# Attention on one core: the value products of a step in one piece of 512 query columns

## The chip, the cores and the metric
The kernel runs on one core of one Trainium2 chip. The metric is the device time of one execution in microseconds (us); of several runs the median is given. One execution was recorded by the hardware profiler, and its times are the ones read below.

## What is computed
Two layers, each an attention over a fixed context and a mixture of experts, all with a residual connection:

```python
x = x + L0_xattn(layernorm(x), ctx, ctx, 16)          # rotary positions, ALiBi bias
x = x + L0_ffn(layernorm(x), ...)                     # top-1 of 8 experts
x = x + L1_xattn(layernorm(x), ctx, ctx, Wq, bq, ...) # with projections
x = x + L1_ffn(layernorm(x), ...)                     # experts choose their tokens
# in both attentions, for 4 batches of 512 tokens and 16 heads of 16 columns:
attn = softmax(q @ k.T / 4 (+ bias)); out = attn @ v
```

Only the two attentions are touched. For each batch and head the scores are 512 x 512, and `attn @ v` sums over the 512 keys.

## The kernel before
Attention works in 16 slots (4 batches x 4 groups of 4 heads, `SLOTS`) of 4 steps each (`TB`, a block of 128 keys), 64 steps `t` in all. A step has two halves, one for each pair of heads. TensorE's program is one list in order of the steps (L656 to L662). In each half it issues, one behind the other:
- `scores` (L614, "S" later): for a block of 128 keys and all 512 queries the scores of two heads, keys on the partitions, with the rows' maxima taken off by extra rows of the product. Two matmuls on two halves of the array's rows.
- `maxima_scores` (L599, "M"): scores the other way round, queries on the partitions, for the slot that comes 8 steps (`AHEAD`) later. VectorE only takes their row maxima (`maxima`, L806).
- `weigh` (L633, "W"): for step `t - 1` the products of `vaug` (values and a column of ones) with `probs`, for the four heads side by side on four groups of 32 columns of the array, accumulated in `ps_out` over the slot's four steps. In half 0 it does query columns 0 to 255, in half 1 columns 256 to 511. The data are float32, and each such matmul is two pairs of weight load and product in the trace.
- pieces of other jobs that the schedule (`attention_schedule`) puts at this step and this half ("position" 0 or 1): the transposes of the maxima (`m`, L495, position 1 of each step divisible by 4), of the outputs (`o`, L503, position 1 of each step 4s + 7), of the normalized queries (L512, position 1), in layer 1 also the projection of the queries (`job_q1`, L520, both positions) and the output projection (L549, L557). All of them share one PSUM bank, `ps_misc`, and each waits until the one before has been copied out.

ScalarE takes exp of each S unit (L739, 128 x 1024), in order, and behind the second half of steps divisible by 4 it copies `ps_out` to `out_sb` (L745) and then the maxima to `max_t` (L674). VectorE, besides the maxima, negates them at the end of a slot (L812, L813) and divides the outputs (L784, L791).

S and M write to a ring of three units of two PSUM banks in the fixed order S, M, S, M, ... (`ring_schedule`). So each takes the unit of the one three places before (`take_unit`, L572 to L578): an M waits for the exp of the S of the half step before (`exp_done`), an S for the row maximum of the M two half steps before (`mx_read`). `weigh` waits for the second exp of step `t - 1`, and in the first step of a slot for the copy of the slot before (`out_copied`). `probs` has three buffers; an exp waits for the products of three steps before (`pv_done`).

In the first 8 steps (`t` below 0) there are only maxima, in the last 8 (56 to 63) no more maxima. Each stage of the kernel begins when the one before has ended. SyncE issues the loads of queries, keys and maxima, GpSimd the stores of the queries and keys, each waiting for counts of `st_full`, `mx_full`, `misc_free` or `pv_done`.

Of the kernel before, what the change touches and what calls it, by code (L numbers as in the profile page):

```python
# [15 lines left out]
B, T, D = 4, 512, 256  # L16
# [3 lines left out]
TB = T // P  # L20
DC = D // P
FC = F // P
HG = 4
# [3 lines left out]
VW = 32  # L27
# [116 lines left out]
def attention(nc, m, layer, dram):  # L144
# [7 lines left out]
    NV = 2 if layer == 0 else B  # L152
    with ExitStack() as ctx:
        def sb(name, shape, dt):
            return ctx.enter_context(nc.sbuf_tensor(f"a{layer}_{name}", shape, dt))

        def sem(name):
            return m.ctx.enter_context(nc.semaphore(f"a{layer}_{name}"))
# [3 lines left out]
        probs = sb("probs", [P, 3, HG, T], F32)  # L162
        vaug = sb("vaug", [P, NV, TB, H, VW], F32)
# [44 lines left out]
        vaug_set = sem("vaug_set")  # L208
# [14 lines left out]
        exp_done = sem("exp_done")  # L223
        v_ready = sem("v_ready")
        pv_done = sem("pv_done")
        out_copied = sem("out_copied")
# [80 lines left out]
        with nc.Block() as block:  # L307
# [182 lines left out]
            def _(pe):  # L490
# [73 lines left out]
                def piece(job, n):  # L564

                    if n == 0 and index[job] and not (layer == 1 and job in first):
                        pe.wait_ge(misc_free, index[job])
                    ins = run[job[0]](job, n)
                    if n == last_piece.get(job[0], 0):
                        ins.then_inc(misc_full, 1)  # L570
# [9 lines left out]
                def maxima_scores(n):  # L580

                    if not 0 <= n < 2 * STEPS:
                        return
                    s, w = n // 8, n % 8
                    p, qt = w // TB, w % TB
                    b, g = s // NG, s % NG
                    for part in range(2 if b else 3):
                        if w == 0 and g == groups(b, part)[0]:
                            if s == 0:
                                pe.wait_ge(first_loaded, 64)  # L590
                            else:
                                pe.wait_ge(loaded[part if b else part - 1], 64 * (b + 1))
                            if s in row_pieces:
                                piece = row_pieces.index(s)
                                pe.wait_ge(rows_in[piece % 2], 32 * n_kinds * (piece // 2 + 1))
                    to = take_unit("m", n)
                    for par in range(2):
                        rows = slice(par * HALF_P, par * HALF_P + M_ROWS)
                        ins = pe.matmul(to[:, par], qa[rows, b % 2, g, p, qt * P:(qt + 1) * P], ka[rows, b % 2, g, p], start=True, stop=True)  # L599
                    ins.then_inc(mx_full, 1)  # L600

                def scores(n):

                    if not 0 <= n < 2 * STEPS:
                        return
                    t, p = n // 2, n % 2
                    s, kc = t // TB, t % TB
                    b, g = s // NG, s % NG
                    if kc == 0 and p == 0:
                        pe.wait_ge(max_in[s % 2], 32 * (s // 2 + 1))  # L610
                    to = take_unit("s", n)
                    for par in range(2):
                        rows = slice(par * HALF_P, par * HALF_P + S_ROWS)
                        ins = pe.matmul(to[:, par], ka[rows, b % 2, g, p, kc * P:(kc + 1) * P], qa[rows, b % 2, g, p], start=True, stop=True)  # L614
                    ins.then_inc(st_full, 1)

                def weigh(t, half):

                    if not 0 <= t < STEPS:
                        return  # L620
                    s, kc = t // TB, t % TB
                    b, g = s // NG, s % NG
                    cols = slice(half * T // 2, (half + 1) * T // 2)
                    if half == 0:
                        pe.wait_ge(exp_done, 2 * t + 2)
                        if kc == 0:
                            pe.wait_ge(v_ready, b + 1 if layer == 0 else 2 * (b + 1))
                            if layer == 1:
                                pe.wait_ge(vaug_set, 1)
                            if s:  # L630
                                pe.wait_ge(out_copied, s)
                    for h in range(HG):
                        ins = pe.matmul(m.ps_out[VW * h:VW * (h + 1), cols], vaug[:, b % NV, kc, HG * g + h], probs[:, t % 3, h, cols],  # L633
                                        start=(kc == 0 and half == 0), stop=(kc == TB - 1 and half == 1), skip_group_check=True)
                    if half == 1:
                        ins.then_inc(pv_done, 1)

                pe.wait_ge(m.ident_in, 16)
                if layer == 1:
# [16 lines left out]
                for t in steps:  # L656
                    for half in range(2):
                        scores(2 * t + half)
                        maxima_scores(2 * (t + AHEAD) + half)
                        weigh(t - 1, half)  # L660
                        for job, n in pieces.get((t, half), []):
                            piece(job, n)  # L662

            @block.scalar
            def _(act):
                def act_job(job):
                    if job[0] in ("o", "a"):
                        return
                    act.wait_ge(misc_full, index[job] + 1)
                    if job[0] == "m":  # L670
                        s = job[1]
                        if s >= 2:
                            act.wait_ge(max_in[s % 2], 32 * (s // 2))
                        nc.scalar.copy(max_t[:, s % 2], misc[0:2 * MAX_ROWS]).then_inc(misc_free, 1)  # L674
                    elif job[0] == "qt":
                        nc.scalar.copy(xnt[:, job[1] % 2], bank(job)[:].rearrange("p (c t) -> p c t", c=DC)).then_inc(misc_free, 1)
                    elif job[0] == "q":
                        i = job[1]
                        if i >= 2:
                            act.wait_ge(q_ready, max(i - 1, 2))  # L680
                        src = bank(job)[:].rearrange("p (c t) -> p c t", c=DC)
                        if layer == 0:
                            nc.scalar.copy(qx[:, i % 2], src).then_inc(misc_free, 1)
                        else:
                            to = qst[:, i, 0] if i < 2 else qx[:, i % 2]
                            for o in range(DC):
                                ins = nc.scalar.activation(to[:, o], src[:, o], ACT.Identity, bias=bqk[:, 0, o:o + 1])
                            ins.then_inc(misc_free, 1)
                    elif job[0] == "at":
                        _, b, c = job  # L690
                        if b:
                            act.wait_ge(misc_full, index["a", b - 1, 1] + 1)
                        nc.scalar.copy(att_t[:, c], misc[:]).then_inc(misc_free, 1)
# [1064 lines left out]
```

## Time and profile before

| | us |
|---|---|
| runs, median of 3 | 1064.61 (1059.42 to 1065.59) |
| the profiled execution | 1059.8 |
| its span, from the first to the last instruction | 1058.0 |
| TensorE products busy | 951.0 |
| VectorE busy | 596.9 |
| ScalarE busy | 514.3 |
| GpSimd busy | 309.5 |

Busy times are sums over the whole span, and the stages differ in their limits. Products on TensorE overlap in the profile's records, since their ends are modelled, so that the distance between the starts of two groups says more than their lengths. A group of S, M or W in the trace in order of time is one line with its count (x2, x2, x8).

### The profile page before, as it was taken

Reading aid. Unit: us, or ns where it says so; the run is one execution under the profiler, and the core shown is the slowest. Engines: PE = TensorE matmul, PEld = TensorE weight load, DVE = VectorE, ACT = ScalarE, POOL = GpSimd, SP = SyncE. Lnnn points to the kernel's source line nnn. Section 1 sums busy time; section 2 is a strip of 40 time slices with the busy share of each in tenths; the row PEclk is TensorE's granted clock in tenths of the full one; section 3 lists DMA queues with packets and bytes.
Section 4 is the critical chain, followed back from the end, with each engine's and each line's share of the span. In section 5 each row is a group of like instructions: output and inputs, shape, how many; then the busy total and the mean of one; then the engine's idle time right before and its main releaser. Section 6 shows DMA issues by size and latency. Waiting matters only on the chain. (4 is left out here: it accounts for less than half of the span.)

```text
span 1058.0 us, 17516 instructions
## 1 busy us (share of the span) xinstructions
PE 951.0 (90%) x6902; PEld 653.6 (62%) x6902; DVE 596.9 (56%) x1011; ACT 514.3 (49%) x777; POOL 309.5 (29%) x296
## 2 busy tenths in 40 slices
PE   4289999997988999998879999999979999999994
PEld 3134344443858999998634434344349989999994
DVE  7588989981440111110796856869415846655663
ACT  1148777785342323322336765757643044445550
POOL 7597661000001222223042122000001255554222
PEclk9569999999689999999888989989998999999998
DMA  7878555200569999994737161330007225555316
GB/s 249 170 219 226 132 124 108 40 3 20 195 255 352 346 335 350 339 335 153 175 99 147 38 143 41 64 63 3 4 1 242 81 70 133 153 167 136 100 20 179
DMA packets 53045, 158.98 MB, mean 150 GB/s; under 512 B 8272, under 2 KB 28368, under 8 KB 42288
## 3 DMA queue, kind: packets, MB, share of 16 engines
q1 hardware_dynamic: 36464, 121.96, 38.8%
q0 software_dynamic: 13296, 29.63, 10.5%
q10 hardware_dynamic: 3216, 6.43, 1.6%
q8 instruction: 48, 0.79, 0.3%
q14 instruction: 21, 0.17, 0.1%
HBM read 116.18 MB, written 40.76 MB: 148 GB/s over the span
## 5 line engine op out<-in xcount | busy, mean ns | idle before, releaser
L806 DVE TENSOR_REDUCE a_row_max<-ps_ring 128x2 f32<-128x1024 f32 x256 | 308.4, 1221 | 76.9 <-PE ps_ring L599 76.2
L739 ACT ACTIVATE a_probs<-ps_ring 128x1024 f32<-128x1024 f32 x256 | 261.3, 1024 | 99.3 <-PE ps_ring L614 97.9
L633 PE MATMUL ps_out<-a_probs,a_vaug 128*32 128x256 f32 x2048 | 168.3, 402 | 2.5 <-ACT a_out_sb L745 1.5
L599 PE MATMUL ps_ring<-a_ka,a_qa 52*128 52x512 f32 (+1 forms) x512 | 120.8, 475 | 29.4 <-DMA a_ka<-scratch_k_scr 21.4
L614 PE MATMUL ps_ring<-a_qa,a_ka 56*128 56x512 f32 (+1 forms) x512 | 132.3, 513 | 2.3 <-DMA a_qa<-a_max_t 1.2
L1076 ACT ACTIVATE e_hid<-ps_ring,e_wts 128x128 f32<-128x128 f32 x184 | 52.3, 369 | 119.5 <-PE ps_ring L1176 70.0
L614 PEld LDWEIGHTS ps_ring<-a_qa,a_ka 56*128 56x128 f32 (+1 forms) x512 | 49.2, 189 | 97.0 <-issue 68.2
L1465 ACT ACTIVATE e_hr<-ps_ring 128x512 fp32r<-128x512 f32 x64 | 38.3, 599 | 118.2 <-PE ps_ring L1536 118.2
L633 PEld LDWEIGHTS ps_out<-a_probs,a_vaug 128*32 128x32 f32 x2048 | 41.0, 109 | 80.0 <-issue 73.9
L599 PEld LDWEIGHTS ps_ring<-a_ka,a_qa 52*128 52x128 f32 (+1 forms) x512 | 51.8, 200 | 61.7 <-ACT a_probs L739 22.8
L1536 PE MATMUL ps_ring<-e_xt,e_wr 128*128 128x512 f32 x384 | 88.7, 390 | 0.4 <-DVE e_xt L1604 0.4
L1176 PEld LDWEIGHTS ps_ring<-e_xst,e_wts 128*128 128x128 f32 x736 | 87.2, 195 | 2.0 <-issue 0.8
L1176 PE MATMUL ps_ring<-e_xst,e_wts 128*128 128x128 f32 x736 | 87.5, 278 | 0.6 <-DVE e_xst L1275 0.6
L1188 PE MATMUL ps_ring<-e_wts,e_hid 128*128 128x256 f32 x368 | 83.8, 381 | 0.1
L1536 PEld LDWEIGHTS ps_ring<-e_xt,e_wr 128*128 128x128 f32 x384 | 71.6, 188 | 15.1 <-issue 0.6
L1624 DVE TENSOR_TENSOR e_hr<-e_hf,e_hr 128x512 fp32r<-128x512 f32 x64 | 44.4, 694 | 54.5 <-ACT e_hf L1468 54.5
L1188 PEld LDWEIGHTS ps_ring<-e_wts,e_hid 128*128 128x128 f32 x368 | 68.1, 190 | 9.3 <-ACT e_hid L1076 0.8
L1429 POOL DMA_INDIRECT scratch_acc<-e_ys,e_token x32 | 57.1, 1786 | 54.7 <-DVE e_ys L1618 50.8
L1017 POOL DMA_INDIRECT scratch_ys<-e_ys,e_to_row x23 | 22.8, 992 | 122.0 <-DVE e_ys L1284 122.0
L1420 POOL DMA_INDIRECT e_xg<-scratch_xl,e_token x32 | 32.2, 1008 | 75.7 <-PE ps_ring L1520 46.7
L1284 DVE TENSOR_TENSOR e_ys<-ps_ring,e_wts 128x256 f32<-128x256 f32 x23 | 9.8, 424 | 75.4 <-PE ps_ring L1188 75.4
L1281 DVE TENSOR_TENSOR e_xst<-ps_misc,e_rms_t 128x256 f32<-128x256 f32 x22 | 9.3, 424 | 75.4 <-PE ps_misc L1157 75.4
(231 smaller groups left out, 1283.4 us busy)
## 6 DMA issues: line engine op xcount, KB each, us to landing
e_wts<-in_w SPq DMA_DIRECT2D x23, 1156.0 KB, 8.4
e_wts<-in_w SPq DMA_DIRECT2D x23, 1024.0 KB, 8.0
e_wf<-in_w SPq DMA_DIRECT2D x16, 1024.0 KB, 6.1
a_qa<-scratch_q_scr SPq DMA_DIRECT2D x28, 384.0 KB, 8.6
a_ka<-scratch_k_scr SPq DMA_DIRECT2D x28, 384.0 KB, 7.2
scratch_q_scr<-a_qst POOLq DMA_DIRECT2D x36, 256.0 KB, 3.2
scratch_k_scr<-a_kst POOLq DMA_DIRECT2D x9, 512.0 KB, 13.8
scratch_xl<-e_xn SPq DMA_DIRECT2D x8, 512.0 KB, 5.3
```

The costliest lines, as they stand in the source:

```text
L599: ins = pe.matmul(to[:, par], qa[rows, b % 2, g, p, qt * P:(qt + 1) * P], ka[rows, b % 2, g, p], start=True, stop=True)
L614: ins = pe.matmul(to[:, par], ka[rows, b % 2, g, p, kc * P:(kc + 1) * P], qa[rows, b % 2, g, p], start=True, stop=True)
L633: ins = pe.matmul(m.ps_out[VW * h:VW * (h + 1), cols], vaug[:, b % NV, kc, HG * g + h], probs[:, t % 3, h, cols], start=(kc == 0 and half ...
L739: nc.scalar.activation(probs[:, t % 3, 2 * half:2 * half + 2], unit("s", n), ACT.Exp, scale=HD ** -0.5).then_inc(exp_done, 1)
L806: dve.tensor_reduce(row_max[:, s % 3, qt, :, p], unit("m", n), AX.X, ALU.max).then_inc(mx_read, 1)
L1076: nc.scalar.activation(hid[:, k, fc], m.ps_st[:, 2 * k + half, q * P:(q + 1) * P], ACT.Silu, bias=wts[:, k, w1_cols + FC * D + fc:w1_cols ...
L1176: ins = pe.matmul(m.ps_st[:, 2 * k + half, q * P:(q + 1) * P], wts[:, k, c * F + fc * P:c * F + (fc + 1) * P], xst[:, k, c], start=(c == 0 ...
L1188: ins = pe.matmul(m.ps_max[:, k, 0:D], hid[:, k, fc], wts[:, k, w1_cols + fc * D:w1_cols + (fc + 1) * D], start=(fc == 0), stop=(fc == FC ...
L1429: pool.indirect_dma_start(dram["acc"], bass.IndirectOffsetOnAxis(token[:, e, b:b + 1], 0), ys[:, e % 2, b], None, compute_op=ALU.add).then ...
L1465: nc.scalar.activation(hr[:, 0, fc], m.ps_st[:, fc % 4], ACT.Gelu_apprx_tanh)
L1536: ins = pe.matmul(m.ps_st[:, fc % 4], wr[:, k, wp, c * F + fc * P:c * F + (fc + 1) * P], xt[:, xp, c], start=(c == 0 and (wp, xp) == (0, 0 ...
L1624: dve.tensor_tensor(hr[:, 1, fc], hf[:, fc % 4], hr[:, 0, fc].bitcast(F32), ALU.subtract).then_inc(h_split, 1)
```

## The change
The four heads' products of a step are issued once, in the first half of the following step, with all 512 query columns each. In the second half nothing takes their place. The waits are the same and stand where they stood, at the first half. The increment of `pv_done`, which used to come with the last product of the second half, now comes with the last of the first half. The order on TensorE was S M W S M W in a step and is S M W S M.

```diff
-                def weigh(t, half):
+                def weigh(t):
...
-                    cols = slice(half * T // 2, (half + 1) * T // 2)
-                    if half == 0:
-                        pe.wait_ge(exp_done, 2 * t + 2)
-                        if kc == 0:
...
+                    pe.wait_ge(exp_done, 2 * t + 2)
+                    if kc == 0:
...
                     for h in range(HG):
-                        ins = pe.matmul(m.ps_out[VW * h:VW * (h + 1), cols], vaug[:, b % NV, kc, HG * g + h], probs[:, t % 3, h, cols],
-                                        start=(kc == 0 and half == 0), stop=(kc == TB - 1 and half == 1), skip_group_check=True)
-                    if half == 1:
-                        ins.then_inc(pv_done, 1)
+                        ins = pe.matmul(m.ps_out[VW * h:VW * (h + 1)], vaug[:, b % NV, kc, HG * g + h], probs[:, t % 3, h],
+                                        start=(kc == 0), stop=(kc == TB - 1), skip_group_check=True)
+                    ins.then_inc(pv_done, 1)
...
                         scores(2 * t + half)
                         maxima_scores(2 * (t + AHEAD) + half)
-                        weigh(t - 1, half)
+                        if half == 0:
+                            weigh(t - 1)
                         for job, n in pieces.get((t, half), []):
                             piece(job, n)
```

## Rows read from the trace of the kernel before

**Rows 1.** The page, busy time (share of the span) and instructions of TensorE.
```profile
PE 951.0 (90%) x6902; PEld 653.6 (62%) x6902; DVE 596.9 (56%) x1011; ACT 514.3 (49%) x777; POOL 309.5 (29%) x296
```

**Rows 2.** The page's groups by line: busy us, mean ns of one | idle before.
```profile
L806 DVE TENSOR_REDUCE a_row_max<-ps_ring 128x2 f32<-128x1024 f32 x256 | 308.4, 1221 | 76.9 <-PE ps_ring L599 76.2
...
L633 PE MATMUL ps_out<-a_probs,a_vaug 128*32 128x256 f32 x2048 | 168.3, 402 | 2.5 <-ACT a_out_sb L745 1.5
```

**Rows 3.** Stretches: us, busy of each engine, granted clock, DMA share, GB/s.
```profile
200.30:211.96 11.66, 11.66 (x108) 4.74 (x104) 10.55 (x14) 9.14 (x11) 0.73 (x1) 1.00 0.02 4
234.00:255.00 21.00, 19.31 (x190) 7.08 (x188) 2.56 (x9) 17.58 (x20) 2.05 (x3) 1.00 0.02 4
```

**Rows 4.** In order of time (start us, us), layer 0, two half steps.
```profile
205.46 1.02 ACT L739 ACTIVATE a_probs<-ps_ring 128x1024 f32<-128x1024 f32 x1 [0.43 <-PE ps_ring L614]
...
206.15 0.50 PE L614 MATMUL ps_ring<-a_qa,a_ka 56*128 56x512 f32 x2
206.53 0.19 PEld L599 LDWEIGHTS ps_ring<-a_ka,a_qa 52*128 52x128 f32 x2 [0.20 <-ACT a_probs L739]
...
206.69 1.02 ACT L739 ACTIVATE a_probs<-ps_ring 128x1024 f32<-128x1024 f32 x1 [0.21 <-PE ps_ring L614]
...
206.97 0.64 PE L633 MATMUL ps_out<-a_probs,a_vaug 128*32 128x256 f32 x8
...
207.54 0.50 PE L614 MATMUL ps_ring<-a_qa,a_ka 56*128 56x512 f32 x2
...
207.88 0.39 PE L599 MATMUL ps_ring<-a_ka,a_qa 52*128 52x512 f32 x2
...
208.20 0.64 PE L633 MATMUL ps_out<-a_probs,a_vaug 128*32 128x256 f32 x8
```

**Rows 5.** The same view: steps with out transposes (L503) and maxima transposes (L495).
```profile
210.16 0.66 PE L503 MATMUL ps_misc<-ident,a_out_sb 128*128 128x128 f32 x4
...
210.74 0.50 PE L614 MATMUL ps_ring<-a_qa,a_ka 56*128 56x512 f32 x2
...
210.96 0.18 DVE L812 TENSOR_SCALAR a_neg_max<-a_row_max 128x16 fp32r<-128x16 f32 x1
...
211.89 2.34 DVE L806 TENSOR_REDUCE a_row_max<-ps_ring 128x2 f32<-128x1024 f32 x2
...
213.36 0.60 PE L495 MATMUL ps_misc<-ident,a_neg_max 128*8 128x128 f32 x4
213.56 0.59 ACT L745 COPY a_out_sb<-ps_out 128x512 f32<-128x512 f32 x1
...
213.90 0.50 PE L614 MATMUL ps_ring<-a_qa,a_ka 56*128 56x512 f32 x2
```

**Rows 6.** The same view: last eight steps of layer 0.
```profile
234.50 0.64 PE L633 MATMUL ps_out<-a_probs,a_vaug 128*32 128x256 f32 x8
...
241.62 0.64 PE L633 MATMUL ps_out<-a_probs,a_vaug 128*32 128x256 f32 x8
242.19 0.19 PEld L614 LDWEIGHTS ps_ring<-a_qa,a_ka 56*128 56x128 f32 x2 [0.41 <-issue]
...
242.74 1.02 ACT L739 ACTIVATE a_probs<-ps_ring 128x1024 f32<-128x1024 f32 x1 [0.17 <-PE ps_ring L614]
...
253.55 1.07 PE L633 MATMUL ps_out<-a_probs,a_vaug 128*32 128x256 f32 x16
```

**Rows 7.** The same view: a step of layer 1 with the query projection.
```profile
642.24 1.13 PE L520 MATMUL ps_misc<-a_xnt,a_wq 128*128 128x256 f32 x4
...
644.30 0.66 PE L503 MATMUL ps_misc<-ident,a_out_sb 128*128 128x128 f32 x4 [0.93 <-ACT a_qx L687]
```

**Rows 8.** The same view: the first value products of layer 0.
```profile
68.32 1.08 PE L633 MATMUL ps_out<-a_probs,a_vaug 128*32 128x256 f32 x8
69.33 0.79 PE L614 MATMUL ps_ring<-a_qa,a_ka 56*128 56x512 f32 x2
```

More of the change, by code:

```diff
@@ L622, in weigh @@
                     b, g = s // NG, s % NG
-                    cols = slice(half * T // 2, (half + 1) * T // 2)
-                    if half == 0:
-                        pe.wait_ge(exp_done, 2 * t + 2)
-                        if kc == 0:
[L627 to L631, printed above, removed]
+                    pe.wait_ge(exp_done, 2 * t + 2)
+                    if kc == 0:
+                        pe.wait_ge(v_ready, b + 1 if layer == 0 else 2 * (b + 1))
+                        if layer == 1:
+                            pe.wait_ge(vaug_set, 1)
+                        if s:
+                            pe.wait_ge(out_copied, s)
                     for h in range(HG):
-                        ins = pe.matmul(m.ps_out[VW * h:VW * (h + 1), cols], vaug[:, b % NV, kc, HG * g + h], probs[:, t % 3, h, cols],
-                                        start=(kc == 0 and half == 0), stop=(kc == TB - 1 and half == 1), skip_group_check=True)
-                    if half == 1:
-                        ins.then_inc(pv_done, 1)
+                        ins = pe.matmul(m.ps_out[VW * h:VW * (h + 1)], vaug[:, b % NV, kc, HG * g + h], probs[:, t % 3, h],
+                                        start=(kc == 0), stop=(kc == TB - 1), skip_group_check=True)
+                    ins.then_inc(pv_done, 1)
                 pe.wait_ge(m.ident_in, 16)
```

## The prediction
> **What bounds the kernel now.** I read the page's busy shares first: TensorE is busy 90% of the 1058.0 us span [rows 1]. The groups by line come next: the four heads' value products of L633 and the row maxima of L806 are among the costliest [rows 2], and both belong to the two attention layers. Only these are touched, so the rest of the reading is of their steps. A stretch of exactly four steps late in layer 0 is 11.66 us long, has TensorE busy all through and VectorE for 10.55 us, and the granted clock is 1.00 in it, the upper of the two levels, 2.4 GHz [rows 3]. That is 2.91 us a step.
>
> A busy TensorE is not yet one that sets the pace, so I went to the instructions in order of time [rows 4]. I call the score products of L614 S, the maxima products of L599 M, the value products of L633 W. A half step is S, M, W. The distances between starts are S to M 0.34 (207.54 to 207.88), M to W 0.32 (207.88 to 208.20), W to the next S 0.57 (206.97 to 207.54): 1.23 us. Every second half step has M held back: at 206.53 its weights are loaded, released by the exp of the S before, which ran from 205.46 to 206.48. Such a half step takes S to M 0.38 and M to W 0.44, 0.16 more. A step without other work is thus 2 x 1.23 + 0.16 = 2.62. Four of them, the out transposes (0.58, 210.16 to 210.74) and the maxima transposes (0.54, 213.36 to 213.90) [rows 5] make 11.60, against 11.66 seen. So TensorE sets the pace, in order, and one wait just begins to show: with three units in the ring, M of a half step writes where the S of the half step before was, and must wait for its exp.
>
> That wait is the one to watch. exp starts 0.54 after its S (206.15 to 206.69), takes 1.02, and M's load follows 0.05 behind its end: **1.61 us** from an S to the M it releases. Today S, M, W and the next S fill 1.23 + 0.34 = 1.57 of it, so that only 0.04 shows directly, and 0.12 because M's weights can't be loaded ahead.
>
> **The change, part by part.**
>
> *The products themselves.* Of W's 16 pairs of load and product a step, 8 of double width remain. No row shows four heads side by side at 512 columns. Bound from above: two separate pieces, 2 x 0.57 = 1.14. Nearest row: at 253.55 all 16 pairs run with nothing between, in 1.07 [rows 6] against 0.64 for 8 [rows 4]. So a second piece adds 0.43, and the fixed part is 0.57 - 0.43 = 0.14. Bound from below: the streaming alone, 0.86. The 16 pairs cost 0.57 + 0.43 = 1.00; I take 0.99 for the wide piece, which has half the loads, since these lay beside products already. TensorE's work falls by 2 x 0.57 - 0.99 = 0.15 us a step.
>
> *The order.* A step becomes S0, M0, W, S1, M1, then the next S0, M0. Between S1 and the next M0 there is no W: S1 to M1 0.34, M1 to S0 0.32, S0 to M0 0.34, 1.00 us in place of 1.57, while S1's exp still takes 1.61. So in each plain step M0 is held by 0.6 us, and W, behind it in the queue, too. The loop is M0 to W 0.44, W to S1 0.99, S1 to M0 1.61: **3.04 us** against 2.62, +0.42. M1 isn't held: it follows S1, 1.4 us behind M0, when the exp of S0 is long over.
>
> *What the gap hides.* Pieces at position 1 of `piece` lie between M1 and the next S0, in those 0.6 us. They cost their full length before. A step with the out transposes stands at +0.42 - 0.58 = -0.16 (only W's saving is left). VectorE then has the negated maxima and the division between two row maxima, 0.93 (210.96 to 211.89) [rows 5]. It is done with M1's maximum 3.42 after M0 (M1 at 1.77, start 0.43 later, 1.22 long [rows 2]), begins the next at 4.35 and ends it at 5.57; the S0 that needs this comes at 5.13 without it, so at 5.62, and its M0 0.38 later at 6.00, still ahead of 6.08 where its exp ends. No cost, with 0.08 to spare. A step with the maxima transposes: +0.42 - 0.54 = -0.12. But the copy of L745 stands on ScalarE behind S1's exp, 0.59 long [rows 5], and the next W needs its end, about 0.14 later than W would come otherwise: +0.14, so +0.02.
>
> *Steps 1 to 55 of each layer.* Layer 0: 25 plain x 0.42 = 10.5; 13 with maxima transposes x 0.02 = 0.3; 13 with out transposes and 4 with query transposes x -0.16 = -2.7. Less 0.8 for the 0.06 by which 11.60 falls short of 11.66 in 14 groups, and less 1 for the first two steps, in which the clock is at 1.2 GHz, a piece of W takes 1.08 [rows 8] and TensorE's own work covers the exp: +6.3. Layer 1 has the query projection too, 1.13 of work in each half of a step, and waits between pieces such as the 0.93 ahead of 644.30 [rows 7]. Where that work is, the new wait is covered. 22 plain x 0.42 = 9.2; 8 x 0.02 = 0.2; 10 with out transposes and 15 full ones x -0.16 = -4.0; less 0.8; less 2 for some five steps at the low clock: +2.6.
>
> *Steps 56 to 63, without maxima.* From the W at 234.50 to that at 253.55 are 19.05 us for 8 steps. A plain one is W to S 0.57 (241.62 to 242.19), S to exp 0.55, exp 1.02, next W 0.05: 2.19 [rows 6]. With W in one piece it is 0.99 + 0.55 + 1.02 + 0.05 = 2.61. Eight are 20.9; twice the copy of L745 stands between the exp and the W that needs both, +0.55 each; the transposes are hidden. 22.0 against 19.05: +2.95 a layer, 5.9 for both. The next stage begins behind the layer's last instruction, so all of it counts.
>
> **Sum:** 6.3 + 2.6 + 5.9 = +14.8 us. No DMA is moved past another: SyncE and GpSimd wait for counts of S, M and W that come within a microsecond of before, and the load of the maxima has three steps to land. The profiled execution took 1059.8 us, so the sum gives 1074.6. The median of the runs, 1064.6, is 4.8 above it; from there it is 1079.4. I take the middle, **1077 us**.
>
> **Rivals.**
> *A, TensorE stays the bound and the change wins.* If M0's wait were covered, 0.15 us would be saved in each of 126 steps: -19, 1041 on the profiled time, 1046 on the median: 1043. For it: TensorE busy in all of 11.66 us. Against: M's load is released by an exp in today's trace already. It decides where the loop of M0, W, S1 and exp is no longer than TensorE's own work of 2.62 - 0.15 = 2.47 a step, that is if the 1.61 were under 1.04. The Trainium skill, page Perfetto Trace Analysis, section Matmuls, says that larger matmuls are more efficient than smaller ones where possible; by that rule alone the time would come out as here. The trace agrees as to the 0.14 that each piece costs beside its columns, not as to what waits for it.
> *B, no change.* W takes its streaming alone, 0.86: the loop is 2.91, and 0.13 less in 126 steps is -16: -2 in all, 1058 to 1063. Within 1% it is as long as W is under 0.95.
> *C, more is late.* W costs 1.14: 0.15 x 126 = 19 more, 1096. Or the copy, the cast and the row maxima add 0.25 to 0.5 in each of 27 groups of four steps, as the 0.08 to spare is used up: 7 to 13 more, 1084 to 1090.
> *D, the clock falls.* TensorE would be at work for 2 x 0.34 + 0.99 = 1.67 of 2.61 us in the last steps, 64%; today it is for 1.82 of 2.19 and the clock is 1.00 [rows 3]. At 1.2 GHz a piece of W holds the engine for 1.01 (68.32 to 69.33) in place of 0.57, and S is 0.79 long, not 0.50 [rows 8]; the wide piece would be 0.99 x 1.01 / 0.57 = 1.75. With S1 0.29 longer and M0 0.2, the loop grows by 1.25 a step: 16 steps give +20, 1097.
>
> **From these to the numbers.** Forecast 0.58 (itself 1070 to 1085), A 0.07, B 0.13, C 0.15, D 0.07. The range 1060 to 1092 leaves out A, D and the upper end of C. About 1% is what a measurement of this kernel tells from no change, here 1054 to 1075. Slower by over 1%: three quarters of the forecast, C and D, 0.66. Within 1%: the rest of the forecast and B, 0.27. Faster: A, 0.07.
>
> **What would show it.** Four steps late in layer 0 take 12.2 to 12.4 us (4 x 3.04 + 0.14), not 11.66. In plain steps the load of M0 starts 0.05 behind an exp, and M0 about 0.95 behind S0 instead of 0.34; M1 is not held; W to S1 is 0.95 to 1.0; both transposes lie in the gap and the loop is no longer with them than without; the last steps are 2.6 apart. W to S1 below 0.9 would make B right; an M0 that no exp releases, A; a clock of 0.5 in the last steps, D.

## The result and the profile after
The changed kernel is slower: 1087.7 us median (1082.9 to 1091.0) against 1064.6 (1059.4 to 1065.6), ratio 1.024 with a 95% interval of 1.019 to 1.029. Measured twice more, beside the kernel before on the same chip each time, it gave 1.0165 (1.013 to 1.020) and 1.018 (1.015 to 1.021). The three together are about +1.95%, or +20.7 us. Runs more than 1.5% above the fastest of their kernel, which also had a lower mean clock, are left out of the ratios.

The page of the changed kernel, with the rows that answer to [rows 1, 2], and below it the one row of the kernel before that is needed beside them:

```profile
span 1089.1 us, 15468 instructions
...
PE 935.9 (86%) x5878; PEld 635.7 (58%) x5878; DVE 596.3 (55%) x1011; ACT 506.0 (46%) x777; POOL 309.9 (28%) x296
...
L804 DVE TENSOR_REDUCE a_row_max<-ps_ring 128x2 f32<-128x1024 f32 x256 | 307.3, 1221 | 95.0 <-PE ps_ring L599 93.0
...
L599 PE MATMUL ps_ring<-a_ka,a_qa 52*128 52x512 f32 (+1 forms) x512 | 121.0, 475 | 55.3 <-ACT a_probs L737 27.9
L631 PE MATMUL ps_out<-a_probs,a_vaug 128*32 128x512 f32 x1024 | 142.3, 628 | 12.9 <-ACT a_probs L737 8.1
```

```profile
L599 PE MATMUL ps_ring<-a_ka,a_qa 52*128 52x512 f32 (+1 forms) x512 | 120.8, 475 | 29.4 <-DMA a_ka<-scratch_k_scr 21.4
```

TensorE's work has fallen, from 951.0 to 935.9 us, and W's from 168.3 to 142.3, but the span grew by 31.1. TensorE is idle for 55.3 us ahead of M (L599), where it was 29.4, and the exp (L737) ends 27.9 of that; before, what ended most of it was a load of the keys. A smaller busy time with a longer span says that the work saved was not what the time hung on.

Four steps late in layer 0 of the changed kernel, by busy time (us, busy of PE, its weight load, DVE, ACT, POOL, granted clock, DMA share, GB/s), answering to [rows 3]; they begin and end at an S:

```profile
207.28:219.70 12.42, 11.10 (x76) 4.05 (x73) 10.56 (x14) 8.80 (x10) 0.74 (x1) 1.00 0.02 4
```

TensorE has 1.3 us of idle time in them, where it had none in 11.66. By the exps, whose starts mark a period more evenly, four such steps are 12.36. The instructions in order of time show where it sits, one plain step of the changed kernel, answering to [rows 4]:

```profile
212.52 1.06 PE L631 MATMUL ps_out<-a_probs,a_vaug 128*32 128x512 f32 x8
...
213.51 0.50 PE L614 MATMUL ps_ring<-a_qa,a_ka 56*128 56x512 f32 x2
...
213.85 0.40 PE L599 MATMUL ps_ring<-a_ka,a_qa 52*128 52x512 f32 x2
...
214.06 1.94 ACT L737 ACTIVATE a_probs<-ps_ring 128x1024 f32<-128x1024 f32 x2 [1.11 <-PE ps_ring L614]
214.09 0.39 PE L614 MATMUL ps_ring<-a_qa,a_ka 56*128 56x512 f32 x2
...
215.13 0.51 PE L599 MATMUL ps_ring<-a_ka,a_qa 52*128 52x512 f32 x2 [0.66 <-ACT a_probs L737]
...
215.57 1.06 PE L631 MATMUL ps_out<-a_probs,a_vaug 128*32 128x512 f32 x8
```

S1 starts at 213.51, its exp at 214.06, and M0 can begin at 215.13 only, 0.66 after TensorE was ready. W stands behind M0 in the queue and starts at 215.57. From W to W it is 3.05: 0.99 to S1, 1.62 to M0, 0.44 to W.

### The profile page after: what moved, and what is told of

The parts are those of the page before. It is cut to its first block and busy times, and to the rows that moved or that the text cites. A ratio compares the mean times of both kernels' runs of the same rounds, so it can differ in the third digit from the quotient of the medians.

```text
span 1089.1 us, 15468 instructions
## 1 busy us (share of the span) xinstructions
PE 935.9 (86%) x5878; PEld 635.7 (58%) x5878; DVE 596.3 (55%) x1011; ACT 506.0 (46%) x777; POOL 309.9 (28%) x296
## 5 line engine op out<-in xcount | busy, mean ns | idle before, releaser
L737 ACT ACTIVATE a_probs<-ps_ring 128x1024 f32<-128x1024 f32 x256 | 257.2, 1023 | 136.2 <-PE ps_ring L614 135.8
L599 PE MATMUL ps_ring<-a_ka,a_qa 52*128 52x512 f32 (+1 forms) x512 | 121.0, 475 | 55.3 <-ACT a_probs L737 27.9
L631 PE MATMUL ps_out<-a_probs,a_vaug 128*32 128x512 f32 x1024 | 142.3, 628 | 12.9 <-ACT a_probs L737 8.1
L614 PE MATMUL ps_ring<-a_qa,a_ka 56*128 56x512 f32 (+1 forms) x512 | 125.6, 494 | 5.1 <-DVE a_row_max L804 3.6
L599 PEld LDWEIGHTS ps_ring<-a_ka,a_qa 52*128 52x128 f32 (+1 forms) x512 | 51.8, 199 | 95.5 <-ACT a_probs L737 54.8
L631 PEld LDWEIGHTS ps_out<-a_probs,a_vaug 128*32 128x32 f32 x1024 | 20.9, 109 | 51.0 <-issue 33.1
```

The source lines that it names most:

```text
L631: ins = pe.matmul(m.ps_out[VW * h:VW * (h + 1)], vaug[:, b % NV, kc, HG * g + h], probs[:, t % 3, h], start=(kc == 0), stop=(kc == TB - 1) ...
L737: nc.scalar.activation(probs[:, t % 3, 2 * half:2 * half + 2], unit("s", n), ACT.Exp, scale=HD ** -0.5).then_inc(exp_done, 1)
```

## The experiments
Kernels named "wide" have W in one piece; those named "halves" have it in two. All ratios are against the kernel before, run on the same chip. "Four steps" is the mean distance of four steps over steps 36 to 51 of layer 0, by the starts of the exps; "the last eight" is the time from the first exp of step 56 to the end of the last exp of step 63, in layer 0 too. For the kernel before it is 18.9, for the changed one 21.9.

**The two kernels again.** No edit: first the kernel before, then the changed one.

> The kernel before, unchanged, profiled once more, to see how far the stages that the change does not touch differ from one execution to the next. Theory 1 (chance of the execution): the two mixtures of experts, 165.5 and 202.1 us long in the first profile of before, come out up to 3 us longer or shorter here, and the clock of an attention's first steps rises up to 3.4 us earlier or later. Theory 2 (a consequence of the change): they come out as before within 0.5 us, and only kernels with the wide piece show the 168.1 and 208.2 us.

> The changed kernel, unchanged, with its time and one more profile. Both theories: four steps late in layer 0 take 12.3 us, the wide piece is 0.99 from its start to the next score products, M0's load follows an exp. Theory 1: mixtures of experts 165 to 168 and 202 to 208, not tied to the kernel; time 1084 to 1090. Theory 2: 168 and 208 again.

Measured: before 1066.6 us (one run; 1064.7 is the median of 17 beside it), four steps 11.64, the last eight 18.86. Changed 1083.6, ratio 1.0165 (1.013 to 1.020); four steps 12.36, the last eight 24.2, with the clock at its lower level in steps 62 and 63.

The first pair of profiles differed by 31.1 us, of which 12.0 lay outside both attentions (each taken from its first exp to its last), in code that is the same. From the start of layer 1's last W to the end it was 278.8 us in the first profile of the kernel before and 285.8 in the second, and 287.8 and 286.9 in the changed kernel. Over thirteen profiles that stretch went from 278.8 to 290.2, and the one from layer 0's last W to layer 1's first exp from 291.3 to 298.4, with either form of W at both ends. So nothing ties the 12.0 to the change: executions of either kernel differ by as much, and only the steps themselves are compared below.

**Is it the width of the products or their place?** Both pieces of 256 columns, but one right behind the other at the first half:

```diff
-                        weigh(t - 1, half)
+                        if half == 0:
+                            weigh(t - 1, 0)
+                            weigh(t - 1, 1)
```

> The change's place without its size: the two pieces of 256 columns stay, but both are issued in the first half. Theory (the place costs, as M0 has to wait for S1's exp): the pair takes 1.00, the loop 3.05, four steps 12.3 to 12.4, the time within 0.3% of the changed kernel's. Rival (the width costs, a product of 512 columns over four column groups streams slower or holds back what is behind it): the time within 0.5% of the kernel before.

Measured: 1080.1 us, ratio 1.019 (1.013 to 1.025); four steps 12.38, the last eight 21.91. In order of time, this kernel:

```profile
192.91 1.07 PE L633 MATMUL ps_out<-a_probs,a_vaug 128*32 128x256 f32 x16
...
193.91 0.49 PE L614 MATMUL ps_ring<-a_qa,a_ka 56*128 56x512 f32 x2
...
195.52 0.50 PE L599 MATMUL ps_ring<-a_ka,a_qa 52*128 52x512 f32 x2 [0.60 <-ACT a_probs L741]
```

Sixteen narrow pairs hold TensorE for 1.00 us (192.91 to 193.91), eight wide ones for 0.99. The width is worth 0.01 us a step; in the steps the whole loss is in the place, and so is the saving of 0.15, since it comes whenever two pieces stand next to each other.

**The piece at the second half.** From the changed kernel:

```diff
-                        if half == 0:
+                        if half == 1:
                             weigh(t - 1)
```

> The wide piece of step t - 1 in the second half, behind S1 and M1, instead of the first: S0 M0 S1 M1 W. Theory (M waits 1.61 us for the exp of the S before, and the gap this opens is only worth something where pieces lie in it): the loop is M1, W, S0, exp, M1 and again 0.44 + 0.99 + 1.61 = 3.04, but the transposes of the second half now stand between W and S0, on the loop, and cost their 0.58 and 0.54: four steps 12.16 + 1.12 = 13.3, against 12.35 of the changed kernel, about 25 us more in all, 1105 to 1112. Rival (the loss is one of the wide piece itself): the time within 0.5% of the changed kernel's.

Measured: 1103.7 us, ratio 1.0385 (1.033 to 1.044); four steps 13.37, the last eight 16.60, less than in either kernel. In order of time, this kernel:

```profile
200.20 0.49 PE L599 MATMUL ps_ring<-a_ka,a_qa 52*128 52x512 f32 x2 [0.65 <-ACT a_probs L737]
...
200.63 1.07 PE L631 MATMUL ps_out<-a_probs,a_vaug 128*32 128x512 f32 x8
...
201.62 0.66 PE L503 MATMUL ps_misc<-ident,a_out_sb 128*128 128x128 f32 x4
...
202.21 0.50 PE L614 MATMUL ps_ring<-a_qa,a_ka 56*128 56x512 f32 x2
...
203.83 0.50 PE L599 MATMUL ps_ring<-a_ka,a_qa 52*128 52x512 f32 x2 [0.64 <-ACT a_probs L737]
```

Now W (200.63) and the transposes (201.62) stand in one half, and the other half still has its wait of 0.64 for the exp. What W's place decides is which half is left empty. With W at the first half the gap takes the transposes in; with W at the second it takes in nothing.

**M behind W.** If M0 holds W back, W could be put ahead of it. It must then be that of step t - 2, since the exp of t - 1 isn't over; the copy of `ps_out` goes one step later. From the changed kernel:

```diff
                         scores(2 * t + half)
+                        if half == 0:
+                            weigh(t - 2)
                         maxima_scores(2 * (t + AHEAD) + half)
-                        if half == 0:
-                            weigh(t - 1)
...
-                        if half == 1 and t >= TB and t % TB == 0 and t // TB <= SLOTS:
+                        if half == 1 and t >= TB and t % TB == 1 and t // TB <= SLOTS:
```

> The wide piece works on step t - 2 and stands between S0 and M0; the copy of the outputs moves one step later with it. Nothing then waits for an exp that is not long over: from S1 to the next M0 there are 2.0 us of work. Theory (a ring of three units is short of time, whichever of its waits is met): the next S0 waits for the row maximum of M0, 0.44 + 1.22 + 0.05 behind it, then 0.44 to W and 0.99: a loop of 3.14, with the delay of VectorE at a slot's end 12.8 for four steps; the last eight steps, where there are no maxima, fall to 2.0 to 2.1 each: 1083 to 1092 us. Rival (only M0's wait for exp cost time): four steps come down to VectorE's 10.7 and the kernel is faster than before, 1035 to 1045.

Measured: 1096.1 us, ratio 1.032 (1.025 to 1.038); four steps 13.26, a plain step 3.25 to 3.42, the last eight 19.19. In order of time, this kernel:

```profile
208.60 0.50 PE L599 MATMUL ps_ring<-a_ka,a_qa 52*128 52x512 f32 x2
...
209.15 2.35 DVE L804 TENSOR_REDUCE a_row_max<-ps_ring 128x2 f32<-128x1024 f32 x2 [1.07 <-PE ps_ring L599]
...
210.43 0.50 PE L614 MATMUL ps_ring<-a_qa,a_ka 56*128 56x512 f32 x2 [0.85 <-DVE a_row_max L804]
210.85 1.06 PE L631 MATMUL ps_out<-a_probs,a_vaug 128*32 128x512 f32 x8
...
211.85 0.50 PE L599 MATMUL ps_ring<-a_ka,a_qa 52*128 52x512 f32 x2
```

The wait for an exp is gone and another has taken its place: S at 210.43 is released by a row maximum that began at 209.15, and M0 at 211.85 comes 3.25 after the M0 at 208.60. W makes M0 late, M0's row maximum ends late, and the S that writes there waits. In this order the ring's other wait takes over, and it costs more than the 12.8 that were expected; whether some third order would do wasn't tried. The last eight were to fall to 2.0 to 2.1 a step. A plain step there is 1.81, but twice W waits for the copy of the outputs, 1.46 and 1.63 us, and the eight together gain nothing.

**A cut that isn't even.** From the kernel before, with `weigh` taking its first and last column: 384 columns at the first half and 128 at the second.

```diff
-                        weigh(t - 1, half)
+                        cut = 3 * T // 4
+                        if half == 0:
+                            weigh(t - 1, 0, cut)
+                        else:
+                            weigh(t - 1, cut, T)
```

> One size changed: query columns 0 to 383 in the first half, 384 to 511 in the second. Theory (loop = 2.05 + the first piece, which is 0.14 + 0.43 for each 256 columns): first piece 0.79, a plain step 2.83, between 2.62 and 3.04; four steps 11.9 to 12.1, last steps 2.4: 1073 to 1078 us. Rival (the wait appears only with one undivided piece): 2.62, the time of the kernel before.

Measured: 1070.2 us, ratio 1.007 (1.004 to 1.010); four steps 11.70, the last eight 20.35 and a plain one of them 2.40. In order of time, this kernel:

```profile
191.96 0.49 PE L599 MATMUL ps_ring<-a_ka,a_qa 52*128 52x512 f32 x2
...
192.38 0.85 PE L633 MATMUL ps_out<-a_probs,a_vaug 128*32 128x384 f32 x8
...
193.16 0.50 PE L614 MATMUL ps_ring<-a_qa,a_ka 56*128 56x512 f32 x2
...
194.78 0.18 PEld L599 LDWEIGHTS ps_ring<-a_ka,a_qa 52*128 52x128 f32 x2 [0.41 <-ACT a_probs L743]
194.78 0.49 PE L599 MATMUL ps_ring<-a_ka,a_qa 52*128 52x512 f32 x2
```

M0 to M0 is 2.82 us (191.96 to 194.78), between 2.62 and 3.04, and S1 to M0 is 1.62 again (193.16 to 194.78). W with 384 columns holds the engine 0.78. The loop of M0 to W, W to S1, S1 to M0 gives 0.42 + 0.78 + 1.62 = 2.82. The same sum gives 3.04 with the 0.99 of W whole and 2.62 with the 0.57 of a half, where it is M1 that is held: it fits all three cuts. The four steps came out 0.2 to 0.4 shorter than expected, since a step behind one with transposes doesn't wait, and the whole time came out 3 us below the 1073 to 1078 expected.

**One piece only where something fills the gap.** If the gap is what costs, W in one piece should gain in those steps where a transpose stands at the second half. From the kernel before, with `weigh` taking its first and last column:

```diff
-                        weigh(t - 1, half)
+                        cut = T if (t, 1) in pieces and t < STEPS - AHEAD else T // 2
+                        if half == 0:
+                            weigh(t - 1, 0, cut)
+                        elif cut < T:
+                            weigh(t - 1, cut, T)
```

> The wide piece only in those steps, up to step 55, in whose second half another job's piece is scheduled; elsewhere two halves as before. Theory (a gap of 0.6 us opens behind S1 and pays only where a transpose fills it): two plain steps 2.62 each, two steps with transposes 3.04 and 3.18, so 11.46 for four in place of 11.66, 0.2 less in 27 groups and some 0.2 more in each step with a query or output projection: 5 to 8 us faster than the kernel before, 0.5 to 0.7%. Rival (the wide piece costs wherever it stands): slower than before by half of what the change costs, about 1%.

Measured: 1065.1 us, ratio 1.0015 (0.999 to 1.004); four steps 11.83, the last eight 18.85. Four steps should have been 11.46. In order of time, this kernel, in the step behind maxima transposes:

```profile
200.99 0.58 ACT L749 COPY a_out_sb<-ps_out 128x512 f32<-128x512 f32 x1
...
201.93 1.92 ACT L743 ACTIVATE a_probs<-ps_ring 128x1024 f32<-128x1024 f32 x2
...
202.99 0.50 PE L599 MATMUL ps_ring<-a_ka,a_qa 52*128 52x512 f32 x2 [0.21 <-ACT a_probs L743]
```

In steps divisible by 4 ScalarE copies the outputs and casts the maxima behind S1's exp. The next exp starts only at 201.93, and the M at 202.99 waits for it. So in these steps the gap on TensorE is filled but ScalarE isn't free. The step behind them takes 3.18 from M0 to M0, although its own W is in halves, where the kernel before took 2.69. The same edit without them:

```diff
-                        cut = T if (t, 1) in pieces and t < STEPS - AHEAD else T // 2
+                        cut = T if (t, 1) in pieces and t % TB and t < STEPS - AHEAD else T // 2
```

> As the mixed kernel, but steps divisible by 4 keep their halves: there the copy and the cast on ScalarE hold back the exps behind them, and the mixed kernel paid 0.43 us. Theory: the wide piece stays where out or query transposes fill the gap, 0.16 less in 26 steps and about 0.2 in some 12 others: 5 to 7 us faster than the kernel before at the same clock, 0.5 to 0.7%. Rival (what a wide step gains, the next gives back): within 0.2% of the kernel before.

Measured: **1056.3 us** (1051.6 to 1060.0, 11 runs), ratio 0.9935 (0.991 to 0.996); four steps 11.41, the last eight 18.89. In order of time, this kernel, a step with the out transposes:

```profile
184.84 1.07 PE L633 MATMUL ps_out<-a_probs,a_vaug 128*32 128x512 f32 x8
...
186.38 1.03 ACT L743 ACTIVATE a_probs<-ps_ring 128x1024 f32<-128x1024 f32 x1 [0.64 <-PE ps_ring L614]
...
186.50 0.66 PE L503 MATMUL ps_misc<-ident,a_out_sb 128*128 128x128 f32 x4
...
187.09 0.49 PE L614 MATMUL ps_ring<-a_qa,a_ka 56*128 56x512 f32 x2
...
187.55 0.49 PE L599 MATMUL ps_ring<-a_ka,a_qa 52*128 52x512 f32 x2
```

The transposes at 186.50 lie where S1's exp runs (186.38 to 187.41), so that the M at 187.55 comes 0.46 behind its S and not 1.04 as in a plain step of the changed kernel (214.09 to 215.13). Four steps fell by 0.25. Of this 0.15 is W's own saving. Most of the rest is that M1 isn't held in such a step, since W stands whole between S0 and S1: from S1 to M1 and on to what follows it is 0.34 and 0.33, where the kernel before has 0.38 and 0.44. This version beats both kernels, by 0.65% the one before.

**Free M from S's ring.** How much of the loss hangs on the shared ring shows when it is taken away. Rings of their own, two units for S and two of one bank for M, fit in PSUM only if M is half as large. From the kernel before, the changed kernel, and the changed kernel with `weigh(t - 2)` and the copy a step later:

```diff
-            r = 2 * (place[kind, n] % 3)
+            if kind == "m":
+                return ring[:, 4 + n % 2:5 + n % 2]
+            r = 2 * (n % 2)
...
-                        pe.wait_ge(mx_read if was == "m" else exp_done, k + 1)
+                    if n >= 2:
+                        pe.wait_ge(mx_read if kind == "m" else exp_done, n - 1)
...
-                    for par in range(2):
+                    for par in range(1):
```

> Units apart: scores have two units of two banks, maxima two units of one bank. For that only one of the two maxima products is made (VectorE reads its bank twice, so its time is the same), and exp multiplies its input by zero, so that all values stay finite. The value products are in halves, as before. M no longer waits for an exp nor S for a row maximum. Expected by all: the wait behind every second S is gone, 2.46 a step, four steps 10.9 to 11.0 in place of 11.66.

> The same units apart and the same parts left out (one of two maxima products, exp of zero), with the wide piece in the first half. Theory (the change lost because M0 had to wait for S1's exp): what is left is W's own wait for that exp, a loop of 0.99 + 1.61 = 2.60, four steps 11.0 to 11.1: nearly the halves' 10.95, where with the shared ring there were 0.7 between them. Rival (the wide piece itself): 0.7 us more than with halves again, 11.6.

> As the kernel with units apart and the wide piece, but the piece works on step t - 2, so that it waits for no exp either. Theory: no wait is left but VectorE's eight maxima and 0.93 for a slot's end: 10.7 us for four steps, 0.25 less than with halves: the saving of 0.15 a step shows at last, as far as VectorE lets it. Rival: as much as with halves or more.

These kernels leave out one of the two maxima products of each half (VectorE reads its bank twice in place of it) and take exp of zero, so their whole times (1076, 1063 and 1059 us, one run each) say nothing beside the others, and their steps are compared among the three alone. Four steps: halves 10.99, wide 11.33, wide a step later 11.10. In order of time, first two W a step apart of the wide kernel, then one of the later kernel:

```profile
190.69 1.06 PE L631 MATMUL ps_out<-a_probs,a_vaug 128*32 128x512 f32 x8 [0.40 <-ACT a_probs L737]
...
193.31 1.07 PE L631 MATMUL ps_out<-a_probs,a_vaug 128*32 128x512 f32 x8 [0.40 <-ACT a_probs L737]
```

```profile
194.31 1.06 PE L631 MATMUL ps_out<-a_probs,a_vaug 128*32 128x512 f32 x8 [0.85 <-ACT a_out_sb L743]
```

The loss of wide against halves falls from 0.70 to 0.34 in four steps, and a plain step is 2.62, not 3.04. So about half of the loss in the steps goes with the ring. What is left is W's own wait: even with M free it waits 0.40 for S1's exp, which S1, pushed behind W, starts late. I had expected 11.0 to 11.1 for wide. The later kernel was to show 10.7, and showed 11.10, as W then waits for the copy of the outputs on ScalarE (0.85). That a wide W can win in every step, with both waits gone, wasn't shown.

**The clock.** In all four profiles with W joined at the first half (three of the wide kernel and that of the two pieces together) the clock falls in the last steps of layer 1, at step 59 or 62, in two of them in those of layer 0 too, and in step 53 of layer 1. The wide kernel with rings of its own does it too, at steps 59 and 53. It happens in none of the four profiles with W in halves at these steps (twice the kernel before, both mixed). At steps 21 and 37 of layer 1 the clock falls in some profiles with either form of W (both in the first of the kernel before, 37 in the second of the changed one), so there it belongs to the execution. Two stretches of layer 1, the changed kernel, columns as above:

```profile
761.00:765.00 4.00, 3.32 (x18) 1.27 (x16) 0.97 (x1) 2.20 (x3) 0.00 (x0) 0.63 0.06 12
...
785.90:789.30 3.40, 3.40 (x14) 1.14 (x14) 0.00 (x0) 1.58 (x2) 0.00 (x0) 0.51 0.02 5
```

The third number from the end is the clock, 0.63 and 0.51 of full speed, the second being the lower level, 1.2 GHz. The step at the first took 7.68 us against 5.83 in the kernel before, by the exps of S1; that at the second took 3.75 against 2.61 in the changed kernel's second profile, where the clock hadn't fallen yet. The idle time alone doesn't settle it: the last steps of layer 0 have the same gaps, and in two of the four profiles the clock stays at its upper level in them. To see whether the idle time brings this on, products were repeated in the gap (S0 again, in each step that has no transposes ahead of it), from the changed kernel:

```diff
-                    for par in range(2):
...
+                    again = 0 if p or not t or (t - 1, 1) in pieces else 2 if t > STEPS - AHEAD else 1
+                    for _ in range(1 + again):
+                        for par in range(2):
...
```

> The changed kernel with the first score products of a step issued twice, one behind the other, in steps that follow no piece, and three times in the last steps: 0.32 us of work each in a gap that is empty. The computation is the same. Theory (the gap leaves TensorE with too little to do and the clock falls more often than before): plain steps stay at 3.04 and last steps at 2.6, and the falls of the clock in steps 52 to 54 of layer 1 and 59 to 62, seen in all three profiles with the wide or joined pieces, are gone; 2 to 3 us faster than the changed kernel. Rival (chance): the falls come again at the same places, time as the changed kernel's.

> The changed kernel once more, for comparison with the filled one on the same chip. Theory (its gaps make the clock fall more often): TensorE is at the low clock some 10 us longer in a run than in the filled kernel, and the time is 4 to 6 us more. Rival (chance of the chips): both differ by less than 2 us.

> The changed kernel with the first score products issued twice in plain steps, three times in the last ones. Theory: 1076 to 1080 us where the changed kernel takes 1083, as the low clock holds for a shorter time; plain steps again 3.04. Rival: the changed kernel's time within 2 us, the same time at the low clock.

Measured: filled 1.014 (1.009 to 1.019) on one chip; on another the changed kernel 1.018 (1.015 to 1.021) and filled 1.017 (1.015 to 1.019). Four steps are 12.36 in all three, and the last eight 21.87 and 21.89 filled, 23.17 wide with a fall in them. So the filling is hidden, as meant, and in both filled profiles the last steps of both layers are without a fall, but step 53 of layer 1 has it still (7.64 and 7.78 us), and each has falls elsewhere (at step 17 of layer 0 in one, from steps 20 and 36 of layer 1 in the other). The whole time is the same within the error: 4 to 6 us were expected, the medians differ by 2.0, and each ratio is uncertain by 2 to 3 us. So that the filling brings back a part of the loss isn't shown, and not excluded either. That the idle time decides where in the last steps the clock falls is made likely by two profiles against four, not shown.

## Why the prediction came out so
The sign and the mechanism were right, the size was not. 1077 is 12.4 us over the kernel before; the first comparison gave 23.1, the two repeats 18.9 and 19.7. The medians 1087.7, 1083.6 and 1079.6 all lie inside 1060 to 1092 and over 1% above the kernel before. Of the 10.7 by which the first comparison passes the forecast, 2.4 are the base, 1.7 the sum, all of it in layer 1, and 6.6 stand in no step. By the prediction's own steps, taking for each step the shorter of two profiles of each kernel so that a fall of the clock in one doesn't count (the two rows on transposes by the starts of M0):

| | predicted | measured |
|---|---|---|
| W in one piece, to S1 | 0.99 | 0.99 |
| S1 to M0 | 1.61 | 1.62 |
| plain step | 3.04 | 3.04 |
| four steps late in layer 0 | 12.2 to 12.4 | 12.36 |
| step with out transposes | -0.16 | -0.16 to -0.06 |
| step with maxima transposes | +0.02 | -0.03 |
| layer 0, up to step 55 | +6.3 | +6.2 |
| layer 0, last eight | +2.95 | +3.0 |
| layer 1, up to step 55 | +2.6 | +4.9 |
| layer 1, last eight | +2.95 | +2.4 |
| sum | +14.8 | +16.5 |

*The loop* held term by term, and so did the sum for layer 0. The Trainium skill, page Perfetto Trace Analysis, section Matmuls, says that larger matmuls are more efficient than smaller ones where possible. In this trace that holds for the engine's busy time (15.1 us less) and not for the kernel's time, by the wait of 0.66 us at 215.13. Rival A fell with that wait; B fell with W at 0.99, above its 0.95, and so did the first part of C, W at 1.14.

*The last steps* run as the sum had it. In order of time, the changed kernel, answering to [rows 6]:

```profile
242.99 1.07 PE L631 MATMUL ps_out<-a_probs,a_vaug 128*32 128x512 f32 x8
...
248.78 1.07 PE L631 MATMUL ps_out<-a_probs,a_vaug 128*32 128x512 f32 x8 [0.88 <-ACT a_probs L737]
...
251.39 1.06 PE L631 MATMUL ps_out<-a_probs,a_vaug 128*32 128x512 f32 x8 [0.88 <-ACT a_probs L737]
...
265.03 1.06 PE L631 MATMUL ps_out<-a_probs,a_vaug 128*32 128x512 f32 x8 [0.53 <-ACT a_probs L737]
```

A plain one is 2.61 (248.78 to 251.39), as predicted, and all eight, from W to W, 22.04 (242.99 to 265.03) against 22.0. In layer 1 the loss is some 0.5 smaller, because step 56 holds part of the output projection there and takes 5.83 in both kernels, where the one of layer 0 grew by 0.43.

*The step that failed* is the term of the 15 "full" steps of layer 1, taken at -0.16 each because "Where that work is, the new wait is covered"; the layer's sum up to step 55 came out +4.9 where +2.6 was counted. With the base it accounts for 4.1 of the 10.7 us; the rest stays open. It is covered where the query projection stands: such a step fell from 6.14 to 6.04. It isn't where the output projection stands (its transposes, L549, in steps 20, 36 and 52, its products, L557 before, from steps 22, 38 and 54). Step 36 of layer 1 in order of time, the kernel before (its second profile) and then the changed one:

```profile
685.46 0.50 PE L614 MATMUL ps_ring<-a_qa,a_ka 52*128 52x512 f32 x2
...
686.68 0.50 PE L614 MATMUL ps_ring<-a_qa,a_ka 52*128 52x512 f32 x2
...
688.26 0.59 ACT L745 COPY a_out_sb<-ps_out 128x512 f32<-128x512 f32 x1
...
689.37 0.66 PE L549 MATMUL ps_misc<-ident,a_att 128*128 128x128 f32 x4 [0.69 <-ACT a_max_t L674]
...
691.29 0.50 PE L614 MATMUL ps_ring<-a_qa,a_ka 52*128 52x512 f32 x2
```

```profile
699.63 0.51 PE L614 MATMUL ps_ring<-a_qa,a_ka 52*128 52x512 f32 x2
...
701.42 0.50 PE L614 MATMUL ps_ring<-a_qa,a_ka 52*128 52x512 f32 x2
...
702.88 0.58 ACT L743 COPY a_out_sb<-ps_out 128x512 f32<-128x512 f32 x1
...
703.98 0.66 PE L549 MATMUL ps_misc<-ident,a_att 128*128 128x128 f32 x4 [1.28 <-ACT a_max_t L672]
...
705.89 0.51 PE L614 MATMUL ps_ring<-a_qa,a_ka 52*128 52x512 f32 x2
```

From S1 (686.68 and 701.42) to the next S0 it is 4.61 and 4.47: a chain through ScalarE and back (exp, copy, cast, transpose, copy, transpose) that starts with S1 and in which TensorE has nothing but the transposes to do. S0 to S1 went from 1.22 to 1.79, and 0.43 of this is that W now stands between them whole. The step is 6.26 in place of 5.83, +0.43 where -0.16 was counted. Any work whose start hangs on S1's exp moves with S1; only work that TensorE does itself fills the gap. In the slot of steps 36 to 39 the four steps changed, by the exps, by +0.42, -0.08, +0.33 and -0.30, together 16.30 to 16.67, +0.37, where one plain step at +0.42 and three at -0.16 were counted, -0.06. Steps 20 to 23, 52 to 55, 24 and 40 deviate likewise, and with the clock left aside this makes 1.7 of the 2.3 that layer 1 was short by. Step 53 adds 1.2: by the exps of S1 it is longer by 1.85 and 1.94 in the two profiles of the changed kernel, steps 21 and 37 with the same pieces by 0.31, and it has the clock at 0.63 shown above. The first four steps took back some of this: they came out 2.8 shorter where 1.9 was counted. How much of that is the change's doing is open: the clock rose 16.7, 6.5 and 5.4 us behind the layer's first exp in the three profiles of the changed kernel, 13.6 and 16.8 behind it in the two of the kernel before.

*"Both transposes lie in the gap"* held, but not "no longer with them than without" in every step. From M0 to M0, steps 36 to 39 take 3.04, 3.18, 3.04 and 3.14. The 3.18 follows the maxima transposes: it is the 0.14 by which the copy makes W late, and the forecast had it. The 3.14 is a step with the out transposes; in every second slot they leave 0.10, and what makes the difference wasn't looked into. With them the four steps changed by 0.70, as the sum had it, so that rival C, which put 0.25 to 0.5 more on each such group, fell too.

*The base.* Half of 4.8 us was given away by taking the middle between the profiled execution and the median. The 17 runs beside the repeat span 1055.5 to 1068.1, so 1059.8 is simply one of the shorter; a sum of differences belongs on the median. 1064.6 + 14.8 = 1079.4, and with +16.5 it is 1081.1.

*Rival D* came true in small. The clock falls in the last steps, where D had placed it by their idle time, but in one stretch of two steps at most and not for sixteen: 1.3 us in one (23.17 against 21.87), 2.3 in another (24.2).

*What stays open.* +16.5 step by step against +20.7 of the ratios. Within each set of runs of one kernel (127 in all) the time grows by some 0.38 us with each us at the lower clock, taken as (1 - mean clock) x 2 x span. Of the runs that the ratios use, the three sets of the changed kernel have 150, 149 and 143 us at it on the mean (14 runs, 147 together), the kernel before 140.5 (57 runs). That makes 2.5 of the 4.2, though the fall at step 53 is in both figures. Which part of this is the change's doing and which is chance isn't settled: single runs of the changed kernel go from 129 to 170 us, and each ratio is uncertain by 3 to 5 us.

## What to carry to other kernels
Where an engine issues in order into a ring of buffers, look for the longest loop of a step (issue, consumer's work, release) beside its busy sum; here the loop set the time. Moving work out of the part of the loop in which a consumer runs cost what it used to cover: 0.57 us of cover against 0.15 of work saved, +0.42. Joining the products paid only in the steps where other work of the same engine took the vacated place and the consumer wasn't busy with something else: deciding it per step turned +2% into -0.65%. Before calling a step "covered", see whether the work there is the engine's own or a chain through another engine that starts behind the piece that moved.

## What the hardware showed that I had not expected
- The saving of a joined W doesn't need wide products: 16 pairs of 256 columns in one row take 1.00 us, 8 pairs of 512 take 0.99, two separate groups of 8 take 1.14. A group of W between the products of S and M costs 0.14 beside its columns.
- Untouched stages differ between executions of the same program by as much as the effect looked for: 278.8 to 290.2 us and 291.3 to 298.4. One pair of profiles gave 31 us where the ratios say 21.
- With TensorE idle for 0.88 us in each 2.61 the granted clock fell to its lower level in the last steps of layer 1 in four profiles of four, and with repeated products in that gap in none of two; in those of layer 0, with the same gaps, in two of four. Yet the whole time changed by less than the error (1.018 and 1.017): a fall that is gone in one place isn't yet a gain of the run.
